# Mixture-of-experts layer on one core: zero rows copied from DRAM, the expert table ahead of one shared block, and 24 unread products on TensorE

## The reference, cut to what matters

```python
x = x + xattn(layernorm(x), ctx_1024, ctx_1024, mask, ...)

def ffn(xf):                                  # xf: (4096, 256)
    scores = sigmoid(xf @ gate_weight.T)
    sfc = scores + bias
    # best 4 of 8 groups by their maximum, then the best 6 experts in them
    tw = 2.5 * scores[topk] / scores[topk].sum(-1)
    routed = sum over e of combine[:, e] * ((silu(xf @ gu_e[:128].T) * (xf @ gu_e[128:].T)) @ dn_e.T)
    shared = (silu(xf @ sg.T) * (xf @ su.T)) @ sd.T
    return routed + shared
x = x + ffn(layernorm(x))
```

## Time and profile before

| | us |
|---|---|
| median of 3 runs | 806.86 (806.25 to 812.81) |
| the profiled execution | 811.91 |
| its span, first to last instruction | 809.6 |
| TensorE busy (products) | 734.4 |
| GpSimd busy | 536.7 |
| VectorE busy | 518.8 |
| ScalarE busy | 389.1 |
| mean granted clock of TensorE, of full speed | 0.952 |

### The profile page before, as it was taken

The page is one execution under the profiler, slowest core; times in us unless marked ns, Lnnn a source line. Parts: engine busy times, 40 slices in busy tenths (PEclk is TensorE's granted clock), DMA queues, the critical chain, the costliest instruction groups (busy, mean ns, idle before and its releaser), DMA issues.

```text
span 809.6 us, 18582 instructions
## 1 busy us (share of the span) xinstructions
PE 734.4 (91%) x5770; PEld 650.9 (80%) x5770; DVE 518.8 (64%) x1619; ACT 389.1 (48%) x832; POOL 536.7 (66%) x794
## 2 busy tenths in 40 slices
PE   6899999999999999986389999999989999899970
PEld 3788898889888888853169999899989999788860
DVE  5887777777777777755145334666666686646673
ACT  2454544444444444420026666665555665556540
POOL 0116878788788778867400007688978888778875
PEclk9899999999999999877699999999999999999995
DMA  9223334433333322214566558798978899778872
GB/s 290 78 54 105 125 125 131 131 124 115 114 127 130 126 72 85 79 66 145 183 195 183 173 165 244 220 266 241 288 232 264 246 275 270 224 228 252 255 222 84
DMA packets 113919, 140.27 MB, mean 173 GB/s; under 512 B 17103, under 2 KB 100691, under 8 KB 113824
## 3 DMA queue, kind: packets, MB, share of 16 engines
q1 hardware_dynamic: 90568, 84.75, 34.0%
q0 software_dynamic: 18432, 50.36, 20.4%
q10 hardware_dynamic: 4824, 3.99, 1.5%
HBM read 75.98 MB, written 63.06 MB: 172 GB/s over the span
## 4 chain that ended last, share of the span: by engine, by line
PE 31%; POOL 30%; issue 20%; DVE 11%; another core or an unknown queue 3%; DMA 2%; SPq 1%; ACT 1%; DVEq 0%; POOLq 0%; ACTq 0%
POOL rows L509 19%; PE sc_ps L1007 16%; PE bank L1019 8%; POOL work L499 7%; PE sc_ps L991 4%; POOL rstd L519 2%; DVE work L1464 2%; DVE work L1483 2%; DVE firsts L1041 1%; DMA store<-in_x 1%; POOL work L546 1%; DMA work<-tabd 1%; DVE work L1438 1%; DVE work L1157 1%
## 5 line engine op out<-in xcount | busy, mean ns | idle before, releaser
L1007 PE MATMUL sc_ps<-work 128*128 128x128 f32 x1792 | 221.0, 277 | 4.4 <-issue 1.8
L1007 PEld LDWEIGHTS sc_ps<-work 128*128 128x128 f32 x1792 | 210.3, 193 | 6.9 <-issue 4.5
L546 POOL DMA_INDIRECT work<-yrows,dest x192 | 188.5, 982 | 36.1 <-POOL work L499 20.5
L509 POOL DMA_INDIRECT rows<-work,dest x192 | 187.7, 977 | 35.0 <-issue 34.8
L499 POOL MEMSET work<- 128x304 f32 (+1 forms) x366 | 137.3, 375 | 104.7 <-DMA yrows<-work 88.9
L1438 DVE TENSOR_TENSOR work<-work,sc_ps 128x256 f32<-128x256 f32 x112 | 46.9, 419 | 128.9 <-issue 72.5
L1019 PE MATMUL bank<-wdn,work 128*128 x448 | 116.7, 383 | 9.9 <-issue 5.3
L1019 PEld LDWEIGHTS bank<-wdn,work 128*128 128x128 f32 x448 | 76.5, 191 | 18.2 <-issue 12.3
L688 ACT ACTIVATE work<-bank 128x512 f32<-128x512 f32 x112 | 66.8, 597 | 40.6 <-PE bank L1019 22.5
L1464 DVE SCALAR_TENSOR_TENSOR work<-work 128x256 f32<-128x256 f32 x160 | 76.8, 480 | 10.8 <-DMA work<-yrows,dest 7.5
L596 ACT ACTIVATE work<-work 128x1232 f32<-128x1232 f32 x32 | 39.4, 1231 | 91.9 <-DVE work L1157 75.3
(11 more groups left out here) (168 smaller groups left out, 1105.0 us busy)
## 6 DMA issues: line engine op xcount, KB each, us to landing
work<-rows SPq DMA_DIRECT2D x224, 128.0 KB
yrows<-work SPq DMA_DIRECT2D x224, 128.0 KB
wgu<-in_egu SPq DMA_DIRECT2D x16, 512.0 KB
store<-in_x SPq DMA_DIRECT2D x8, 512.0 KB, 10.6
wdn<-in_edn SPq DMA_DIRECT2D x8, 512.0 KB
out<-work SPq DMA_DIRECT2D x32, 128.0 KB
rows<-work,dest POOLq DMA_INDIRECT x192
work<-yrows,dest POOLq DMA_INDIRECT x192
```

The source lines that it names most:

```text
L509: pool.indirect_dma_start(rows[:, :], bass.IndirectOffsetOnAxis(ap=dest[:, t, k:k + 1], axis=0), rowb[:, m, :], None).then_inc(scat[m], 16)
L546: pool.indirect_dma_start(yg[:, g % RG, :], None, yrows[0:n * P, :], bass.IndirectOffsetOnAxis(ap=dest[:, t, k:k + 1], axis=0)).then_inc(l ...
L1007: last = mm(ps8[2 + m % 2][:, (2 * w + g) * P:(2 * w + g + 1) * P], wst[w][m % 2][:, k * 2 * I + g * I:k * 2 * I + (g + 1) * I], xeT[:, m ...
```

## The change

It has five parts.

1. The 32 tails are copied within DRAM: from the first 128 rows of `rows`, zero since L380, to each start. Both sides are viewed as 16 pieces of 8 KB where there were 128 rows of 1 KB. L380 gets a semaphore of its own, `empty`, for which `store_tails` waits; the count for part 0 goes from 5 to 4.
2. VectorE does s_hidden(7, 0) behind `name_blocks` and `read_table`.
3. SyncE's load of the last down weights, with its wait for the sums of block 6, goes behind the first four loads of rows.
4. TensorE makes WARM = 24 products of the mask (77 x 128, bf16) with `repb` (77 x 308) into a free PSUM bank behind the wait for the table, ahead of the wait for the sums. Nobody reads them.
5. The semaphore `wg_free` and the empty instruction that raised it go; SyncE waits for `bo_parts` instead.

```diff
+WARM = 24
...
         def store_tails(eng, engine, part):
             need(eng, "tail_rows", 0)
+            eng.wait_ge(S_["empty"], 16)
...
-                eng.dma_start(rows[bass.ds(r, P), :], padrow[:, :]).then_inc(tails_st[min(part, 2)], 16)
+                eng.dma_start(rows[bass.ds(r, P), :].rearrange("(a b) d -> a (b d)", a=16),
+                              rows[0:P, :].rearrange("(a b) d -> a (b d)", a=16)).then_inc(tails_st[min(part, 2)], 16)
...
-            sp.dma_start(rows[0:P, :], padrow[:, :]).then_inc(tails_st[0], 16)
+            sp.dma_start(rows[0:P, :], padrow[:, :]).then_inc(S_["empty"], 16)
...
-                    need(sp, "wg_free", 0)
+                    sp.wait_ge(S_["bo_parts"], 9)
...
-            for s in range(SE, SB - 1):
-                need(sp, "base", s - SE, 2)
-                ld_down(E - NX + 4 * (s - SE))
             sp.wait_ge(S_["table"], 2)
             for q in range(3):
-                sp.wait_ge(tails_st[q], 16 * ((5, 6, 22)[q]))
+                sp.wait_ge(tails_st[q], 16 * ((4, 6, 22)[q]))
...
             for j in range(RX):
                 ld_tile(j)
+                if j == 3:
+                    for s in range(SE, SB - 1):
+                        need(sp, "base", s - SE, 2)
+                        ld_down(E - NX + 4 * (s - SE))
...
             pe.wait_ge(S_["table"], 2)
+            for i in range(WARM):
+                mm(ps8[1][:, 0:HCOLS], maskb[:, 0:P], repb[:, :], start=True, stop=True)
             pe.wait_ge(S_["base"], 2 * (SB - SE))
...
-                v.nop().then_inc(S_["wg_free"], 1)
...
             s_hidden(SE, 1)
-            s_hidden(SE + 1, 0)
             name_blocks()
             read_table()
+            s_hidden(SE + 1, 0)
```

More of the change, by code:

```diff
@@ L277, in build @@
         for name in ("ld_const ld_k ld_v ld_q ld_o ld_egu ld_edn ld_mask k_ps kbd_ready v_ps vrows vchunk_ps vbd_ready "
-                     "top_ends bo_parts mask_ready repb_ready pad_ready probs_zero wg_free stats1_ready "
+                     "top_ends bo_parts mask_ready repb_ready pad_ready probs_zero stats1_ready "
                      "gap mean1_ready norm1_ready tmp_ready var1_ready rstd1_ready "
@@ L282, in build @@
                      "gate_add score sfc group expert sel rank place dest selcum "
-                     "counts tail_rows cum_ps fresh pos_ps sch tab tab_st tab_ld bc_ld named sch_ps table yaddr dest2 "
+                     "counts tail_rows cum_ps fresh pos_ps sch tab empty tab_st tab_ld bc_ld named sch_ps table yaddr dest2 "
                      "ld_s up_ps th hidt dn_ps sbase sg_ps shg shh sy_ps base wnorm "
```

## The result

The change made the kernel slower: 817.1 us median of four runs (814.4 to 821.2) against 807.0 of the kernel before, ratio 1.0105, 95% interval 1.0055 to 1.0154. On another chip it came out again as 1.0085 (1.0047 to 1.0124), on a third as 0.9976 (0.9941 to 1.0010), no loss there. Some executions of every kernel take 1 to 2% longer than its others; the ratios leave them out, the medians in the tables do not, and where the text gives two differences of medians, the first leaves them out too. The profiled execution took 814.7 us with a span of 812.5, which is 2.9 us more than the span of before; the runs without a profile show two to three and a half times that.

A forecast was written before the change was run, and what follows sets the result against it. TensorE, busy 91% of the span, was taken as the bound, with the expert stage's start setting the end. Transposes 1.5 us sooner plus 1.5 us of clock make 3.0: 806.86 - 3.0 = 803.9 us, range 793 to 809.

The forecast's parts named there:

- The slow stretch: From 384 to 400 us every engine but GpSimd slows; a tail store's register operation takes 0.69 us; assumed to stay.
- Naming and table: On VectorE, naming of blocks starts at 387.5 at the latest instead of 401.10; table written at 401.3 instead of 407.27.
- None of it on the path while 0.69 us rules there: In the tails' two queues, the copies' issue saving of at most 2.6 us was claimed not to shorten the path.
- Half 1 wants the tanh of 402.83: On VectorE, block 7's second half waits for ScalarE's tanh, kept at 402.83, so it starts at 403.45, ends at 404.85.
- 32 copies of 16 pieces save at most 32 x 0.08 = 2.6 us: Tail issue on two queues: a copy priced at 0.27 us against a store's 0.35, saving at most 2.6 us.
- The landing, "0.5 us on top": Last tails land at 409.1, the stores' own 408.6 plus 0.5 us, before SyncE's first load of rows.
- Down products of block 7, 5.2 us: On TensorE ahead of the experts: first eight at half clock, 5.2 us in all, ending at 410.7 instead of 413.47.
- 24 products, 3.1 us long, clock back for 1.5: On TensorE before the first expert transposes: 3.1 us at full clock; keeping the clock up gains 1.5 us behind them.
- not the later one: VectorE's way to the first laid weights, ready at 415.5, was claimed earlier than TensorE's transposes, ready at 416.8.
- the first (the stores make the stretch): Tail stores cause the slow stretch and copies lift it: 792.6 us, or 799 if half lifted; chance 0.28.
- The second (the stretch costs the unprofiled runs little): The stretch is partly profile writing; without a profile the last scatter bounds both kernels: 806.4 us; chance 0.17.
- The third, that the copies hold the gate: Copies also read DRAM, land late and delay SyncE's first load of rows: 808.6 to 815.6 us; chance 0.10.

The follow-up runs named there:

- a_copy128: The changed kernel with its copies within DRAM made as 128 rows instead of 16 pieces: 818.44 us, ratio 1.0131 to the kernel before.
- a_nowarm: The changed kernel without its 24 unread products, copies kept: 817.01 us, ratio 1.0044 to the kernel before.
- b_order_load: The kernel before with only VectorE's and SyncE's new order (parts 2 and 3): 810.78 us, ratio 0.9975.
- after3: The changed kernel unedited, run again on chip 2: 814.93 us, ratio 1.0085 to the kernel before.
- a_oldtails3: The changed kernel with tails stored from SBUF again instead of copied, on chip 2: 808.48 us, ratio 0.9995 to the kernel before.
- a_oldtails: The changed kernel with tails stored from SBUF again instead of copied, on chip 1: 812.45 us, ratio 0.9957 to the kernel before.
- b_latetails4: The kernel before with all tails stored only behind the last scatter, on chip 8: 819.66 us in one run.
- b_paced4: The kernel before with GpSimd's pause ahead of the last three tiles' scatters too, on chip 8: 802.28 us, ratio 0.9870.
- after_again: The changed kernel unedited, run again on chip 10: 779.40 us, ratio 0.9976 to the kernel before.
- b_warm: The kernel before with the 24 unread products alone, on chip 10: 781.83 us, ratio 0.9998.

## Why the prediction was wrong

I forecast 803.9 us, and 817.1 came, outside the range of 793 to 809. Step by step:

- **The slow stretch stays: right.** Register operations of the tails take 0.70 us from 384 to 400.
- **Naming and table: right in kind.** The naming came at 386.38 (at the latest 387.5 was forecast), the table was written at 402.8 instead of 401.3. "None of it on the path while 0.69 us rules there" was wrong: copies beside the scatters let VectorE go on 5.3 us behind the last one and not 4.2.
- **"Half 1 wants the tanh of 402.83", and "ScalarE's last six tails stand behind the tanh of 402.83, whose time I leave": this step failed.** It came at 405.49. The second half of block 7, its down products and the last tails stand behind it, and it stands behind copies, which I had changed and did not follow on their own queue.
- **"32 copies of 16 pieces save at most 32 x 0.08 = 2.6 us": wrong in sign.** I took the price from a one-piece DMA (0.27 us). A copy costs 0.524, 0.18 more than the store, by its source and not its pieces (a_copy128). Eleven of ScalarE's stand behind the stretch in the changed kernel. The Trainium skill (DMA: Bandwidth & Descriptors, Rules for kernel authors) leaves open, for loads from DRAM into an SBUF tile, whether 16 large or 128 small descriptors are faster. No run here compares the two for such a load; for copies within DRAM this case shows 0.524 us of issue with either.
- **The landing, "0.5 us on top": about right, 0.7.** With issue and tanh the first load came at 413.98 and not at 410.1.
- **Down products of block 7, 5.2 us: 6.44.** I let the clock recover after eight rows; the sixteen took 0.40 each by the mean.
- **24 products, 3.1 us long, clock back for 1.5: right in the trace, not on the path.** 3.14 us from their start to the transposes, and 2.02 instead of 3.49 behind them. But VectorE's way to the laid weights, which I called "not the later one", was: the first expert product, at 419.86, waited 1.02 us for it. And without the products the first sixteen took 2.43 and 3.25 us in the kernels with the new order and stores, so against them the gain is 0.4 and 1.2 us, not 1.5. In the runs the products are worth about nothing.
- **The sum.** At the second pair the change stands 0.02 us ahead of before instead of 3.0. The term that I priced by the wrong row, the copies, is worth 3.3 to 5.2 us at the first load in the profiles and 6 to 7 us in the runs (a_nowarm against b_order_load, after3 against a_oldtails3). Without it the rest of the change gave 0.9957 and 0.9995 (a_oldtails, a_oldtails3), where the forecast was 0.9963.

Of the rivals, the first (the stores make the stretch) fell: copies don't lift it, and b_latetails4 has VectorE's wait without any tail. The second (the stretch costs the unprofiled runs little) fell too: without it b_paced4 gains 5.6 or 8.5 us in unprofiled runs. The third, that the copies hold the gate, is what happened: I had it decide from a landing after 411.2 us or under 145 GB/s, and the copies landed at 412.4 with 149. But the parts of the delay that the profiles show are their issue, the late tanh and the longer stretch, where I had reckoned with the rate; the DMA engines were busy for 42% of the time from 400 to 415. I gave slower by over 1% a chance of 0.07. The row that would have raised it was not in the trace; a bound from above on the unseen issue, twice a store's, would have given an estimate of 12 x 0.35 = 4.2 us on ScalarE's queue behind the stretch and with it the sign.

The first result, of four runs of each kernel, was 1.0105 and the second 1.0085; the two don't differ by their intervals. The profiled execution of before, 811.91 us, stood 5 us over its median, so the two profiles side by side show less of the loss (2.9 us) than the runs. The parts agree roughly with the whole: copies 6 to 7 us, the order 0 to 2 us back, 24 products nothing, makes 4 to 7 us, 0.5 to 0.9%.

## What to carry to other kernels

A DMA's issue time is part of its queue's path: when a transfer is replaced, count its issues up to the next instruction that another engine waits for, and take an unseen kind of DMA as dearer too, not only as cheaper. Don't replace a store from SBUF by a copy within DRAM to save pieces. And when all engines slow down at once, look first at what GpSimd issues without a pause: spacing 18 scatters 0.2 us further apart was worth 0.7 to 1.3% on the one chip with the stretch where it was tried, and nothing (1.0004) on one without; the forecast for the whole change was 0.4%. A result on one chip is not the result on all: compare on more than one.

## What was new of the hardware

- The issue of a copy from DRAM to DRAM takes 0.524 us on ScalarE's queue, with 16 pieces and with 128; the store of the same 128 KB from SBUF 0.34. From the end of the last issue to the first load that waits for it is 2.9 to 3.0 us behind copies and 2.3 behind stores, so it seems to land 0.7 us later.
- On three chips (1, 2 and 8) register operations and DMA issues of tails slow down to 0.7 us each beside scatters issued every 1.27 us, and a wait of VectorE lasts 8 us or more past the product that it waits for (391.2 to 399.4 in b_latetails4). It ends 4.1 to 4.3 us behind the last scatter with stores or nothing beside the scatters (seven profiles), and 5.1 to 6.1 us behind it with copies (six). Beside scatters every 1.49 us there is none of it (chip 8). On chip 10, where the kernel before takes 783 us instead of 809 to 814, there is none of it with scatters every 1.27 us either (after_again, b_warm). What differs between the chips, no run here tells.
- 24 products kept the full clock for the products that followed at once (granted clock 1.00 from 418.5 to 422 us, where the earlier trace rows had 0.51); with 2.38 or 4.09 us of idle time between, the products ran at the half clock as if there had been none. In after_again the granted clock was 1.00 up to 398.2 us, through the idle time, 0.66 from there to 401.0, in the transposes, and 0.50 from 401.0 to 404.8.
